# One-hot rows of a table lookup built from raw ids and a number held in each partition, in a DLRM top tower on Trainium2

## What is computed

```python
e = jnp.stack([tbl_f[ids[:, f]] for f in range(26)], axis=1)        # (512, 26, 128)
all_emb = jnp.concatenate([r_bottom_output[:, None, :], e], axis=1) # (512, 27, 128)
gram = jnp.einsum('bfd,bgd->bfg', all_emb, all_emb)
z = gram[:, TRIU_I, TRIU_J]                                         # 351 products
h = jnp.concatenate([z, r_bottom_output], axis=1)                   # (512, 479)
h = jnp.maximum(h @ W_top1 + b_top1, 0.0)                           # 512
h = jnp.maximum(h @ W_top2 + b_top2, 0.0)                           # 256
y = h @ W_top3                                                      # (512, 1)
```

## Time and profile before

| | us |
|---|---|
| median of 3 runs | 126.03 |
| lowest, highest run | 124.89, 126.24 |
| span of the profiled execution | 126.5 |
| span of the lookups (first to last L720) | 7.6 to 50.8 |
| last gather's start | 100.1 |

### The profile page before, as it was taken

One profiled execution on the slowest core, in us unless ns is written; L12 is line 12 of the kernel. 1 busy time (PEld: TensorE's weight loads), 2 busy tenths in 40 slices (PEclk: granted clock), 3 DMA queues, 4 the chain that ended last, 5 costly groups with the idle time before them and its releaser, 6 DMA issues. The chain is left out here.

```text
span 126.5 us, 3473 instructions
## 1 busy us (share of the span) xinstructions
PE 91.8 (73%) x1395; PEld 73.5 (58%) x1395; DVE 80.7 (64%) x182; ACT 81.8 (65%) x146; POOL 75.5 (60%) x76
## 2 busy tenths in 40 slices
PE   0069889975999969973620864968989897449992
PEld 0048567754788748752510753747776785449971
DVE  1099968996998895465949004896598606983012
ACT  6072999999599699784510592985499525981130
POOL 2078788888789779787777778878777700010000
PEclk9999999999599999997685599599999999995999
DMA  2999997996739993682222222212122200000000
GB/s 67 239 258 228 227 235 158 222 226 188 185 71 241 241 270 69 190 289 51 60 60 55 60 53 62 53 42 67 47 67 62 53 21 5 8 19 0 0 0 1
DMA packets 7001, 14.08 MB, mean 111 GB/s; under 512 B 2027, under 2 KB 2676, under 8 KB 6985
## 3 DMA queue, kind: packets, MB, share of 16 engines
q1 hardware_dynamic: 4632, 9.11, 28.2%
q0 software_dynamic: 2208, 4.48, 14.6%
q10 hardware_dynamic: 144, 0.26, 0.7%
HBM read 13.71 MB, written 0.00 MB: 108 GB/s over the span
## 5 line engine op out<-in xcount | busy, mean ns | idle before, releaser
L313 POOL DMA_INDIRECT emb<-tbl,idx x68 | 74.2, 1091 | 25.3 <-issue 20.4
L720 PE MATMUL pG<-onehot,tab_hi 125*128 125x512 f32 x72 | 21.8, 443 | 10.3 <-ACT tab_hi L473 7.6
L720 PEld LDWEIGHTS pG<-onehot,tab_hi 125*128 125x128 f32 x72 | 14.4, 208 | 15.0 <-ACT tab_hi L473 7.6
L388 DVE TENSOR_SCALAR onehot<-hot 125x512 fp32r<-125x512 int32 x59 | 22.3, 445 | 0.5 <-PE pG L724 0.2
L611 PE MATMUL pT<-ident,emb 128*128 128x128 f32 x68 | 11.4, 297 | 11.5 <-DMA emb<-tbl,idx 11.1
L724 PE MATMUL pG<-onehot,tab_lo 125*128 125x512 f32 x72 | 18.8, 406 | 0.0
L623 PE MATMUL pG<-embT 128*26 128x26 f32 x1024 | 13.5, 199 | 6.7 <-issue 4.9
L461 ACT COPY embT<-pT 128x512 f32<-128x512 f32 (+1 forms) x10 | 10.7, 1065 | 10.9 <-PE pT L611 10.8
L623 PEld LDWEIGHTS pG<-embT 128*26 128x26 f32 x1024 | 11.6, 112 | 9.8 <-issue 7.2
L611 PEld LDWEIGHTS pT<-ident,emb 128*128 128x128 f32 x68 | 8.7, 152 | 13.9 <-DMA emb<-tbl,idx 12.3
L329 DVE COPY embT<-pT 128x512 f32<-128x512 f32 (+1 forms) x10 | 10.3, 1030 | 9.5 <-PE pT L611 9.5
(11 more groups left out here) (69 smaller groups left out, 111.2 us busy)
## 6 DMA issues: line engine op xcount, KB each, us to landing
tab<-tbl SPq DMA_DIRECT2D x8, 448.0 KB
hot<-hot_ids SPq DMA_DIRECT2D x8, 256.0 KB, 4.7
tab<-w SPq DMA_DIRECT2D x7, 256.0 KB, 3.5
emb<-tbl,idx POOLq DMA_INDIRECT x68, 4.1
tab<-tbl SPq DMA_DIRECT2D x9, 52.0 KB
tab<-tbl SPq DMA_DIRECT2D x2, 224.0 KB, 5.6
hot<-hot_ids ACTq DMA_DIRECT2D x1, 256.0 KB, 5.2
bot<-bottom SPq DMA_DIRECT2D x1, 256.0 KB, 6.1
```

Of the source, the lines that this page charges most:

```text
L313: nc.gpsimd.indirect_dma_start(out=emb[:, t % 2, g - LOOKED - 1, :], out_offset=None, in_=tables[f], in_offset=bass.IndirectOffsetOnAxis(a ...
L388: nc.vector.tensor_scalar(hot_rows(i, k), hot[0:VP, i % RING, :], float(k), None, ALU.is_equal).then_inc(s_hotv, 1)
L720: nc.tensor.matmul(pG[i % 2][:, 0, :], tab_hi[:, i % 2, k, :], hot_rows(i, k), start=(k == 0), stop=False)
```

## The change

The ids stay as they are. `id_at` holds p*8+k for all eight k of a partition; DVE converts it once to float (`id_atf`) and negates its last two columns (`minus_id`). A DVE one-hot now compares the raw ids with a column of `id_atf`, an operand read from each partition, in place of a constant. ACT's square takes `minus_id` in place of `minus_k`. The subtraction L383, its semaphore and the two fills of `minus_k` are gone; ACT waits for the landing of the ids (and in lookup 0 for `minus_id`) in place of `s_rel`.

```diff
--- before.py
+++ after.py
@@ -90,9 +90,9 @@
         idx = sb("idx", [128, TILES * TABLES], i32)
         hot = sb("hot", [128, RING, B], i32)
 
-        row0 = sb("row0", [VP, 1], i32)
-        row0f = sb("row0f", [VP, 1])
-        minus_k = sb("minus_k", [VP, 2])
+        id_at = sb("id_at", [VP, VK], i32)
+        id_atf = sb("id_atf", [VP, VK])
+        minus_id = sb("minus_id", [VP, 2])
         tab = sb("tab", [128, RING, VK, D])
         tab_hi = sb("tab_hi", [VP, 2, VK, D], fp32r)
         tab_lo = sb("tab_lo", [VP, 2, VK, D], fp32r)
@@ -137,9 +137,8 @@
         s_b2 = sem("s_b2")
         s_ident0 = sem("s_ident0")
         s_ident = sem("s_ident")
-        s_row0 = sem("s_row0")
-        s_row0f = sem("s_row0f")
-        s_rel = sem("s_rel")
+        s_idat = sem("s_idat")
+        s_idatf = sem("s_idatf")
         s_ones = sem("s_ones")
         s_prod1 = sem("s_prod1")
         s_row = [[sem(f"s_row{t}_{k}") for k in range(len(BANKS))] for t in range(TILES)]
@@ -297,7 +296,7 @@
 
         @block.gpsimd
         def _(pool):
-            nc.gpsimd.iota(row0[:, :], [[0, 1]], base=0, channel_multiplier=VK).then_inc(s_row0, 1)
+            nc.gpsimd.iota(id_at[:, :], [[1, VK]], base=0, channel_multiplier=VK).then_inc(s_idat, 1)
             nc.gpsimd.memset(ident[:, :], 0.0).then_inc(s_ident0, 1)
             pool.wait_ge(s_ident0, 1)
             nc.gpsimd.affine_select(out=ident[:, :], in_=ident[:, :], compare_op=ALU.not_equal, fill=1.0,
@@ -372,20 +371,16 @@
                 nc.vector.scalar_tensor_tensor(out=h2w[:, :], in0=pH2[:, :], scalar=0.0, in1=w3s[:, :],
                                                op0=ALU.max, op1=ALU.mult, accum_out=y[:, t:t + 1]).then_inc(s_y, 1)
 
-            for m in range(2):
-                nc.vector.memset(minus_k[:, m:m + 1], -float(VK - 2 + m))
             nc.vector.memset(ones[:, :], 1.0).then_inc(s_ones, 1)
-            dve.wait_ge(s_row0, 1)
-            nc.vector.tensor_copy(row0f[:, :], row0[:, :]).then_inc(s_row0f, 1)
-            dve.wait_ge(s_row0f, 1)
+            dve.wait_ge(s_idat, 1)
+            nc.vector.tensor_copy(id_atf[:, :], id_at[:, :]).then_inc(s_idatf, 1)
+            dve.wait_ge(s_idatf, 1)
+            nc.vector.tensor_scalar(minus_id[:, :], id_atf[:, VK - 2:VK], -1.0, None, ALU.mult).then_inc(s_idatf, 1)
             for i in range(LOOKED):
                 dve.wait_ge(s_hotids[i], 16)
-                nc.vector.tensor_scalar(hot[0:VP, i % RING, :], hot[0:VP, i % RING, :], row0f[:, :], None,
-                                        ALU.subtract).then_inc(s_rel, 1)
-                dve.wait_ge(s_rel, i + 1)
                 for k in range(dve_tiles(i)):
                     wait_hot_free(dve, i, k)
-                    nc.vector.tensor_scalar(hot_rows(i, k), hot[0:VP, i % RING, :], float(k), None,
+                    nc.vector.tensor_scalar(hot_rows(i, k), hot[0:VP, i % RING, :], id_atf[:, k:k + 1], None,
                                             ALU.is_equal).then_inc(s_hotv, 1)
                 dve.wait_ge(s_tabhi, i + 2)
                 if i >= 2:
@@ -471,13 +466,15 @@
                     else:
                         act.wait_ge(s_tab0_rest, 16)
                     nc.scalar.copy(tab_hi[:, i % 2, k:k + step, :], tab[0:VP, i % RING, k:k + step, :]).then_inc(s_tabhi, 1)
-                act.wait_ge(s_rel, i + 1)
+                act.wait_ge(s_hotids[i], 16)
+                if i == 0:
+                    act.wait_ge(s_idatf, 2)
                 for k in range(dve_tiles(i), VK):
                     n = act_tiles_before(i) + k - dve_tiles(i)
                     if n > 0:
                         act.wait_ge(s_hota, n)
                     nc.scalar.activation(square[:, :], hot[0:VP, i % RING, :], ACT.Square,
-                                         bias=minus_k[:, k - VK + 2:k - VK + 3]).then_inc(s_sq, 1)
+                                         bias=minus_id[:, k - VK + 2:k - VK + 3]).then_inc(s_sq, 1)
                     act.wait_ge(s_sq, n + 1)
                     wait_hot_free(act, i, k)
                     nc.scalar.activation(hot_rows(i, k), square[:, :], ACT.Relu,
```

## The result

The changed kernel has a median of 131.30 us over 4 runs (129.24 to 133.84); the kernel before, now over 4 runs, 126.13 (124.89 to 128.79). The ratio is 1.029, 95% interval 1.022 to 1.036: slower by about 3%. I had said 126.0 within 124.3 to 127.3, and gave "slower" 0.13. (Both kernels have a slower state at a lower granted clock; ratios and intervals leave its runs out and medians keep them, so that a ratio can differ from the quotient of two medians.)

A forecast was written before the change was run, and what follows sets the result against it. The prediction took POOL's chain of gathers up to the 42nd, plus a fixed 56.7 us stretch, as the bound. DVE's net -2.8 us became idle time, so change 0 kept the median, 126.0 us, range 124.3 to 127.3.

The forecast's parts named there:

- What bounds the kernel: PE's transpose of bank (2,1) at 69.80 waits for POOL's 42nd gather; a 56.7 us stretch follows.
- Part 1: Nine L383 subtractions leave DVE, 0.51 us each from start to start: 4.6 us of DVE time gone.
- Part 2: 59 DVE one-hots take their number from a lane: +30 ns each (0 to +60), 1.8 us more DVE.
- Part 3: Worth of DVE's saved time: every tab_lo subtraction catches a gather, wiping out earlier gains or losses; likeliest sum 0.
- Rival (b): With one-hots +60 ns, gathers among them take +0.19 each; one slot lost, +1.25, so 127.3; chance 0.12.
- The rest behind 69.8: The stretch from PE's transpose of bank (2,1) to the end, taken as 56.7 us and untouched by the change.
- (a): One gather slot is gained where gathers race tab_lo starts: -1.25, so 124.8; chance 0.27 together with (d).
- (c): Lane operand loses DVE's fast mode, 59 one-hots 0.27 us longer: +6, so 132; chance 0.03 with the like.
- (d): The lookup chain shifts, gather 12 landing before the tables ahead of it: up to -0.8; chance 0.27 with (a).
- Part 4: At the start, wider iota and copy and one added negation while POOL and DVE idle: cost 0, uncovered 0.3.

The follow-up runs named there:

- constant_no_subtract: The changed kernel with DVE's one-hots comparing raw ids with the constant k, so only the subtraction is removed: 127.53 us, ratio 0.990 against the kernel before.
- the profiled after: First profiled execution of the changed kernel, no edit: span 127.4 us, first to 42nd gather 61.61.
- before_look: A further profile of the kernel before, one execution, no edit: span 125.6 us, first to 42nd gather 58.68.
- before_look2: Another further profile of the kernel before, one execution, no edit: span 124.7 us, first to 42nd gather 59.89.
- after_look: A further profile of the changed kernel, one execution, no edit: span 131.3 us, first to 42nd gather 63.89.

## Why the prediction was wrong

**What bounds the kernel** held: the end follows the 42nd gather. A delay of 2.6 us there cost 2.7; lookups that ended 2.3 later cost nothing.

**Part 1** held in its size and its worth. L383 and its time are gone and gain nothing that shows (constant_no_subtract). DVE's net in the lookup stretch was -1.1, the low end of what I had allowed, since part 2 cost more.

**Part 2 was mis-sized.** I took +30 ns out of 0 to +60 and measured +61 on the spacing (0.335 to 0.396), +66 on the median duration. The median of L383 had it right. I had set it aside as possibly holding waits for POOL's port and took the difference of minima. The one-hots' own minima, 406 and 447, differ by only 41 as well: a minimum is the wrong statistic for a spacing.

**Part 3 is the step that failed**, in the sentence that every tab_lo catches a gather and "wipes out what was gained or lost since the one before". It resets the phase, not the count. tab_lo of lookup 1 caught the 6th gather in three executions of before and the 7th in one; in all four of the change it caught the 5th. At those of lookups 2 and 3 the change is still one gather behind (9th and 12th in all four, against 10th and 13th in three of before and 11th and 14th in one); at that of lookup 4 the profiled after has caught up (16th in both), the other three are at the 14th or 15th. Nor does every tab_lo catch a gather: two of nine let all pass in before_look and in before_look2. At tab_lo of lookup 8 it is the 29th, 31st, 29th and 29th before, the 28th, 32nd, 28th and 26th after (the two high numbers are lookups that ended late).

**Rival (b) was the right mechanism and under-priced.** Its step, +0.19 for each gather among one-hots (1.58 instead of 1.39), came out to the hundredth in undisturbed series: 1.28 long instead of 1.09, 1.58 apart. Over all gathers that start in a one-hot with another behind, it is +0.15. Its price, one slot, 1.25, was too low: 2.5 in the mean of four, 4.0 in after_look. Sorting each chain's gathers by the DVE instruction in which they start, and adding what each lasts beyond 0.944, accounts for it in the means of four. In a one-hot with another behind it: 1.72 before, 3.18 after (ten to fourteen gathers, 1.08 and 1.23 long). In the last one-hot of a series: 0.41 and 1.00; here are the gathers that miss the boundary ahead of tab_lo, which I had not thought of, about 1.2 each where they occur. In tab_lo: 4.59 and 5.65, the one of 2.90 among them. In L383: 0.52 and 0. All others: 1.41 and 1.35. The condition that I gave (+60 ns) was met, and I had given it 0.12 because I trusted +30.

**The rest behind 69.8**, which I held fixed at 56.7, isn't fixed in either kernel: 56.7 to 58.8 before, 57.4 to 59.0 after. Whether the 0.9 between the means of four belongs to the change isn't settled; eleven profiled executions of kernels without the lane operand, edited ones among them, have a mean of 58.2 there, seven with it 58.4.

**Rivals (a), (c), (d)** did not come. **Part 4** held: the first gather started at 5.6 to 6.1 in the four executions of the change, 5.5 to 6.4 before.

## What to carry to other kernels

Removing vector instructions off the path was worth nothing here, and paying for it with something small on each of 59 others cost 3%. The spacing of a series on one engine decided how long the other, which shares its port, waited, in steps of whole instructions. Follow what that adds through the whole series: a later catch resets the phase, not the count. Price an operand by the median of the nearest row, not by its minimum, when a whole series will have it. And before a change of a few per cent is predicted from one profile, take two or three: here one execution's bound stage was 2 us longer than another's, with the same kernel.

## What the runs showed of the hardware

A VectorE comparison of 125x512 with a number held in each partition comes every 0.396 us, with a constant every 0.335; its rate stays the fast one (two-input instructions of the same length take 0.69). The Trainium skill's page "SBUF — State Buffer", section "Who interferes with whom", says that when VectorE is in a 2-port mode, whoever issues first gets the shared pair for the whole instruction and the other fully blocks. The rows agree that a gather blocks, but not that order decides: the gather of 24.00 had been waiting and four later VectorE instructions went ahead of it, each without a pause behind the last. In the kernel before, a waiting gather always got in at the next boundary among one-hots; with the lane operand it sometimes missed one or several. (A miss is not the lane operand's alone: the first gather of constant_no_subtract passed a boundary as well.) A 48-column VectorE memset behind each one-hot cost only 0.01 us of spacing, though it lasts 0.1 by itself, since it overlaps its neighbours.
